# A graph-attention layer on one core: the sum of P1 and P3 taken first on VectorE in every pair of node tiles

## The chip, the core and the metric

The kernel runs on 1 core of a Trainium2 chip. The metric is the device time of one execution in microseconds (us), the median of several runs. Engines are TensorE (PE in the rows, its weight loads PEld), VectorE (DVE), ScalarE (ACT), GpSimd (POOL) and SyncE (SP), which here only issues transfers. Each engine works through its own instructions in order; between engines stand semaphores.

## What is computed

1250 nodes with 1024 features, 40,000 edges. Cut to what matters:

```python
xn = _layernorm(x)                                     # 1250 x 1024
h = xn @ L0_gnn_W                                      # 1024 x 1024: the product of this case
gnn = relu(segment_sum(h[src] * norm[:, None], dst) + b)
q, k = relu(xn @ Wq + bq), relu(xn @ Wk + bk)          # 16 heads of 64
v = xn @ Wv + bv
mix = (q @ (k.T @ v) / (1250 * 64)) @ Wo + bo          # by head; no softmax
x = x + gnn + mix
x = x + ffn(_layernorm(x))                             # quantised gate, up and down products
```

The edges are gathered and summed as a product with a matrix of edge counts. Float32 products are made of three float16 products (high x high, high x low, low x high), so each operand is split into a high half, copied by ScalarE, and a low half, the rest, taken by VectorE.

## The kernel before

The nodes are ten tiles of 128. The stages follow each other on TensorE: K and V products beside the counting of edges, Q products, then `h = xn @ gnn_W`, then Wo, then by tile the aggregation and the mix, then the feed-forward part. The change touches the third only, the stretch from 364 to 465 us.

There two tiles make a pair j (0 to 4, `PAIRS_OF_TILES`), and each pair of 2 x 2 blocks is computed with seven block products instead of eight (Winograd's form of Strassen's scheme). In TensorE's order, with the bank that each adds up in (`b0` to `b3` of `g_bank[j % 2]`, two sets of four for even and odd pairs):

| product | is | bank |
|---|---|---|
| P1 | A11 x B11 | b0, started |
| P2 | A22 x T4 | b2, started |
| P3 | S2 x T2 | b1, started |
| P4 | S1 x T1 | b3, started |
| P5 | A12 x B21 | b0, added |
| P6 | S3 x T3 | b1, added |
| P7 | S4 x B22 | b3, added |

Each is 12 matmuls of 128x512 (line 735) and raises `g_full` by one, so `g_full` reaches 7j + 3 with P3(j). As P5, P6 and P7 add onto banks whose first contents are still wanted by themselves, these are taken away before:

- `keep_p1(j)` (line 1096, ScalarE) copies b0 after P1 into `g_s1` (`p1_kept`); P5 waits for it.
- `u2(j)` (lines 1489 to 1494, VectorE) adds b1 after P3 and `g_s1` into `g_u2` (`u2`). It waits for P3(j), `p1_kept` and for `c12(j-1)`, the last reader of `g_u2`. P6 waits for it, and for the low half of S3.
- `keep_p5(j)` (line 1076, ScalarE) copies b3 after P4 into `g_s5` (`p5_kept`); it waits for P4(j) and for `c22(j-1)`. P7 waits for it.

The sums S1 to S4 of the next pair are made meanwhile. GpSimd's `s1_s3(j+1)` makes S1 and S3 (lines 519 and 522, two times three adds), VectorE's `s2` and `s4` the others (1406, 1408; 1416, 1418). ScalarE's `s_high(j,i)` (line 1060) takes the high half of Si, VectorE's `s_low(j,i)` (line 1423) the low half. After P5 to P7 the results are combined: `u3` (line 1570, needs P6), `c21` (1572), `c12` (1575, needs P7) on VectorE, `c22` (line 542) on GpSimd after `u3`; the four `h_high` (line 1069) on ScalarE and `h_low` (line 1528) on VectorE split the result. A bank of pair j is free for pair j+2 when its `h_low` or `u3` is done. GpSimd works in the order `s1_s3(j+1)`, `c22(j)`; `s1(j+1)` so comes after `c22(j-1)`.

One turn of VectorE's loop for pair j is, before the change: `s_low(j+1,1)`, `s2(j+1)`, `s_low(j+1,2)`, `s_low(j+1,3)`, `u2(j)` (for pair 0 it stands ahead of the loop), `s4(j+1)`, `s_low(j+1,4)`, `h_low` 1, `u3`, `c21`, `c12`, `h_low` 2 to 4. In the last turn, `u2(4)` is followed by the halves of Wo. One turn of ScalarE's: `keep_p1(j)`, `s_high(j+1,1)`, then for pair 0 `keep_p5(0)` and `s_high(1,2)` to `s_high(1,4)`, for the others `s_high(j+1,2)` to `s_high(j+1,4)` and then `keep_p5(j)`; then `h_high` 1 to 4. The order is written out by hand; nothing schedules it. SyncE's queue waits in this stretch for `g_full` 28 (the end of P7(3)) and then loads Wo.

Of the kernel before, what the change touches and what calls it, by code (L numbers as in the profile page):

```python
# [54 lines left out]
def gps_layer(nc, x, src, dst, gnn_W, gnn_b, Wq, bq, Wk, bk, Wv, bv, Wo, bo,  # L55
              clip_x, clip_down, w_gate, w_up, w_down, out):
    with ExitStack() as ctx:
# [208 lines left out]

        pe_slots = [(t + 1, 1) for t in range(6)] + [(6, 3), (7, 1), (8, 1), (9, 1)]
        landed = [16 * sum(1 if kind == "gu" else 2 for kind, _, _ in pieces[i % 2:i + 1:2]) for i in range(len(pieces))]
        PITCH = FB * P

# [676 lines left out]
        def _(act):  # L947
# [108 lines left out]
            def s_high(j, i):  # L1056
                act.wait_ge(SG[f"s{i}"], j + 1)
                if i == 1 and j >= 2:
                    act.wait_ge(S["g_full"], 7 * (j - 1))
                act.activation(s_half[j % 2][:, 2 * (i - 1)], s_sum[i - 1], ACT.Copy).then_inc(SG["s_hi"], 1)  # L1060
# [7 lines left out]
            def h_high(t, half, o):  # L1068
                act.activation(h16[:, half * (K // 2):(half + 1) * (K // 2), t * P:(t + 1) * P],
                               o.rearrange("p (k n) -> p k n", n=P), ACT.Copy, scale=dinv_up[:, t:t + 1]).then_inc(S["h_hi"], 1)  # L1070

            def keep_p5(j):
                act.wait_ge(S["g_full"], 7 * j + 4)
                if j > 0:
                    act.wait_ge(SG["c22"], j)
                act.activation(g_s5, g_bank[j % 2][3][:, :], ACT.Copy).then_inc(SG["p5_kept"], 1)

            def wo_high(n, c):
                act.wait_ge(SM[f"wo_in{n}_{c}"], 16)
                act.wait_ge(S["g_full"], 7 * (PAIRS_OF_TILES - 1) + (7 if n else 3))  # L1080
                act.activation(wo16[n][:, c * (K // 2):(c + 1) * (K // 2), 0, :], wo[n][c], ACT.Copy,
                               scale=W_UP).then_inc(SM["wo_hi"], 1)

            def m_high(i):
                n, p = i // PAIRS, i % PAIRS
                act.wait_ge(SM["prod_full"], i + 1)
                act.activation(m16[0][:, p, n * HALF:(n + 1) * HALF], m_bank[i % 4][:, :], ACT.Copy,
                               scale=1.0 / W_UP).then_inc(SM["m_hi"], 1)

            for j in range(PAIRS_OF_TILES):  # L1090
                last_pair = j == PAIRS_OF_TILES - 1
                b0, b1, b2, b3 = g_bank[j % 2]
                act.wait_ge(S["g_full"], 7 * j + 1)
                if j > 0:
                    act.wait_ge(SG["u3"], j)
                act.activation(g_s1, b0[:, :], ACT.Copy).then_inc(SG["p1_kept"], 1)
                if j + 1 < PAIRS_OF_TILES:
                    s_high(j + 1, 1)
                    if j == 0:
                        keep_p5(0)  # L1100
                    for i in range(2, 5):
                        s_high(j + 1, i)
                if last_pair:
                    wo_high(0, 0)
                if j > 0:
                    keep_p5(j)
                if last_pair:
                    wo_high(0, 1)
                act.wait_ge(S["g_full"], 7 * j + 5)
                act.wait_ge(SM["dinv"], 3)  # L1110
                h_high(2 * j, 0, b0[:, :])
                act.wait_ge(SG["c21"], j + 1)
                h_high(2 * j + 1, 0, b2[:, :])
                act.wait_ge(SG["c22"], j + 1)
                h_high(2 * j + 1, 1, g_c22)
                if last_pair:
                    m_high(0)
                    m_high(1)
                act.wait_ge(SG["c12"], j + 1)
                h_high(2 * j, 1, b3[:, :])  # L1120
# [77 lines left out]
        def _(dve):  # L1198
# [200 lines left out]
            def s2(j):  # L1399

                a11 = [block_at(0, 2 * j, a) for a in range(2)]
                dve.wait_ge(SG["s1"], j + 1)
                if j > 0:
                    dve.wait_ge(SG["s_lo"], 4 * j - 2)
                    dve.wait_ge(SG["s4"], j)
                dve.tensor_tensor(s_sum[1], s_sum[0], a11[0], ALU.subtract)
                dve.drain()
                dve.tensor_tensor(s_sum[1], s_sum[1], a11[1], ALU.subtract).then_inc(SG["s2"], 1)

            def s4(j):  # L1410

                a12 = [block_at(1, 2 * j, a) for a in range(2)]
                dve.wait_ge(SG["s2"], j + 1)
                if j > 0:
                    dve.wait_ge(SG["s_lo"], 4 * j)
                dve.tensor_tensor(s_sum[3], a12[0], s_sum[1], ALU.subtract)
                dve.drain()
                dve.tensor_tensor(s_sum[3], s_sum[3], a12[1], ALU.add).then_inc(SG["s4"], 1)

            def s_low(j, i):  # L1420
                dve.wait_ge(SG["s_hi"], 4 * j + i)
                high, low = [s_half[j % 2][:, 2 * (i - 1) + a] for a in range(2)]
                dve.tensor_tensor(low, s_sum[i - 1], high, ALU.subtract).then_inc(SG["s_lo"], 1)  # L1423
# [65 lines left out]
            def u2(j):  # L1489
                dve.wait_ge(S["g_full"], 7 * j + 3)  # L1490
                dve.wait_ge(SG["p1_kept"], j + 1)
                if j > 0:
                    dve.wait_ge(SG["c12"], j)
                dve.tensor_tensor(g_u2, g_bank[j % 2][1][:, :], g_s1, ALU.add).then_inc(SG["u2"], 1)  # L1494
# [26 lines left out]
            def a_tile(t, par):  # L1521
                dve.tensor_scalar(a_t[par], counts_tile(t), float(COUNT_MAX), None, ALU.min).then_inc(SB["a_ready"], 1)


            def h_low(j, i, t, half, o):
                dve.wait_ge(S["h_hi"], 4 * j + i)
                high, low = [h16[:, a * K + half * (K // 2):a * K + (half + 1) * (K // 2), t * P:(t + 1) * P] for a in range(2)]
                dve.scalar_tensor_tensor(low, o.rearrange("p (k n) -> p k n", n=P), dinv_up[:, t:t + 1], high, ALU.mult,
                                         ALU.subtract).then_inc(S["h_lo"], 1)

            def wo_low(n, c):
                dve.wait_ge(SM["wo_hi"], 2 * n + c + 1)
                high, low = [wo16[n][:, c * (K // 2):(c + 1) * (K // 2), b, :] for b in range(2)]
                dve.scalar_tensor_tensor(low, wo[n][c], W_UP, high, ALU.mult, ALU.subtract).then_inc(SM["wo_lo"], 1)
# [12 lines left out]
            for j in range(PAIRS_OF_TILES):  # L1547
                b0, b1, b2, b3 = g_bank[j % 2]
                more = j + 1 < PAIRS_OF_TILES
                if more:  # L1550
                    s_low(j + 1, 1)
                    s2(j + 1)
                    s_low(j + 1, 2)
                    s_low(j + 1, 3)
                if j > 0:
                    u2(j)
                if more:
                    s4(j + 1)
                    s_low(j + 1, 4)
                else:  # L1560
                    wo_low(0, 0)
                    wo_low(0, 1)
                    dve.wait_ge(SM["wo_lo"], 2)
                    a_tile(0, 0)
                h_low(j, 1, 2 * j, 0, b0[:, :])
                dve.wait_ge(S["g_full"], 7 * j + 6)
                if j > 0:
                    dve.wait_ge(SG["c21"], j)
                    dve.wait_ge(SG["c22"], j)
                dve.tensor_tensor(g_u3, b1[:, :], g_s1, ALU.add).then_inc(SG["u3"], 1)  # L1570
                dve.wait_ge(SG["u3"], j + 1)
                dve.tensor_tensor(b2[:, :], b2[:, :], g_u3, ALU.add).then_inc(SG["c21"], 1)
                dve.wait_ge(S["g_full"], 7 * j + 7)
                dve.wait_ge(SG["u2"], j + 1)
                dve.tensor_tensor(b3[:, :], b3[:, :], g_u2, ALU.add).then_inc(SG["c12"], 1)
                h_low(j, 2, 2 * j + 1, 0, b2[:, :])
                if not more:
                    m_low(0)
                    m_low(1)
                h_low(j, 3, 2 * j + 1, 1, g_c22)  # L1580
                h_low(j, 4, 2 * j, 1, b3[:, :])
# [216 lines left out]
```

## Time and profile before

| | us |
|---|---|
| median of 3 runs | 734.74 |
| the runs | 734.06 to 734.85 |
| the profiled execution | 733.37 |
| its span, first to last instruction | 731.3 |
| TensorE busy in it | 706.8 |
| VectorE, ScalarE, GpSimd busy | 551.0, 233.0, 347.5 |

The span is one profiled execution; 2.07 us of its time lie around the span. A difference is worked out within the profiled execution and then taken from the median. A row of a timeline names the start, the duration, the engine, the line, the operation, what is written and read, how many instructions follow each other, and in brackets the idle time before with what ended it. Rows of the timeline are merged, so that 276 matmuls can stand in one.

### The profile page before, as it was taken

The page shows a single profiled execution, that of the slowest core. Times are in us where ns is not written, and L with a number is a line of the kernel's source. Part 1 is how long each engine was busy: PE and PEld are TensorE (multiplying, and loading weights), DVE is VectorE, ACT ScalarE, POOL GpSimd, SP SyncE. Part 2 cuts the span into 40 slices and gives each one's busy share as a digit, 9 for nine tenths or more (in the row PEclk, how much of TensorE's full clock was granted, in tenths as well). Part 3 has the DMA queues.
Part 4 walks back from the last instruction along what each step waited for, and adds up shares of the span by engine and source line. Part 5 has one row for each costly group of instructions (what it writes and reads, how often), then busy time and mean ns, then how long its engine had stood idle before and what let it go on. Part 6 is the DMA issues. An engine that isn't in the chain of part 4 may idle for free.

```text
span 731.3 us, 11607 instructions
## 1 busy us (share of the span) xinstructions
PE 706.8 (97%) x3801; PEld 363.3 (50%) x3801; DVE 551.0 (75%) x1036; ACT 233.0 (32%) x382; POOL 347.5 (48%) x441
## 2 busy tenths in 40 slices
PE   4999999999999999999997999999999999999996
PEld 2455555545555554566653444444444444445753
DVE  7878887887666778875797674959977778765866
ACT  5133334553332356554323333530100000003431
POOL 4566767898666778865154440011111111113317
PEclk9999999999999999999999899999999999999999
DMA  9752412563000000000000004152322232100607
GB/s 343 220 141 63 109 37 78 158 244 119 0 0 0 1 2 1 1 0 1 1 1 0 1 0 172 59 173 66 76 88 53 55 84 66 34 12 1 116 1 280
DMA packets 52803, 52.27 MB, mean 71 GB/s; under 512 B 36514, under 2 KB 37546, under 8 KB 52752
## 3 DMA queue, kind: packets, MB, share of 16 engines
q1 hardware_dynamic: 52752, 51.61, 23.5%
q8 instruction: 30, 0.49, 0.3%
q14 instruction: 21, 0.17, 0.1%
HBM read 37.96 MB, written 5.12 MB: 59 GB/s over the span
## 4 chain that ended last, share of the span: by engine, by line
PE 75%; DVE 9%; issue 6%; ACT 2%; DMA 2%; POOL 2%; DVEq 1%; POOLq 1%; SPq 0%
PE bank L625 19%; PE bank L862 13%; PE bank L699 12%; PE bank L806 12%; PE bank L735 9%; PE bank L910 3%; PE bank L610 2%; PE bank L939 2%; PE bank L642 2%; DVE counts L1355 2%; PE bank L798 1%; DVE mem L1467 1%; ACT mem L967 1%; DMA mem<-in_L_mix_Wk 1%; POOLq L521 1%
## 5 line engine op out<-in xcount | busy, mean ns | idle before, releaser
L625 PE MATMUL bank<-mem 128*128 128x512 f16 x960 | 224.6, 383 | 2.2 <-ACT mem L967 1.7
L490 POOL TENSOR_SCALAR hot_src<-iota_p,src_col 125x128 bf16<-125x128 bf16 x252 | 186.0, 753 | 14.1 <-issue 14.1
L625 PEld LDWEIGHTS bank<-mem 128*128 128x128 f16 (+1 forms) x960 | 91.3, 98 | 99.6 <-issue 5.6
L1355 DVE TENSOR_TENSOR counts<-bank,counts 128x120 f32 x328 | 92.2, 281 | 41.8 <-PE bank L610 6.6
L862 PE MATMUL bank<-mem 128*128 128x512 f16 (+1 forms) x504 | 105.5, 369 | 0.0
L699 PE MATMUL bank<-mem 128*128 128x512 f16 (+2 forms) x576 | 105.1, 339 | 0.0
L735 PE MATMUL bank<-mem 128*128 128x512 f16 x420 | 93.8, 386 | 4.9 <-DVE mem L1494 4.9
L806 PE MATMUL bank<-mem 128*128 128x512 f16 x400 | 88.0, 379 | 0.2 <-DVE mem L1651 0.2
L862 PEld LDWEIGHTS bank<-mem 128*128 128x128 f16 x504 | 49.3, 98 | 53.7 <-issue 0.3
L699 PEld LDWEIGHTS bank<-mem 128*128 128x128 f16 (+1 forms) x576 | 55.4, 98 | 41.2
L569 POOL TENSOR_TENSOR cols<-cols 128x1 f32<-128x1 f32 x10 | 5.6, 556 | 139.1 <-DVE cols L1678 139.1
L735 PEld LDWEIGHTS bank<-mem 128*128 128x128 f16 x420 | 41.7, 100 | 56.1 <-DVE mem L1423 5.4
L1005 ACT ACTIVATE src_gap<-iota_p,loT 125x128 bf16<-125x128 bf16 x84 | 33.5, 399 | 107.8 <-PE bank L610 99.1
L806 PEld LDWEIGHTS bank<-mem 128*128 128x128 f16 x400 | 39.1, 98 | 47.4 <-issue 0.7
L487 POOL COPY src_col<-loT 125x3 f32 (+1 forms) x84 | 37.4, 445 | 47.6 <-PE bank L610 42.7
L1342 DVE TENSOR_TENSOR hot_dst<-iota_w,keyT 125x480 bf16<-125x480 bf16 x84 | 55.3, 659 | 0.0
L560 POOL TENSOR_TENSOR mem<-mem 128x1024 f32<-128x1024 f32 x10 | 23.5, 2350 | 24.7 <-DMA mem<-in_L_mix_bo 24.7
L1667 DVE SCALAR_TENSOR_TENSOR mem<-bank,mem 128x512 f32<-128x512 f32 (+1 forms) x21 | 14.0, 666 | 27.6 <-PE bank L862 26.7
L610 PEld LDWEIGHTS bank<-hot_dst,hot_src 125*128 125x128 bf16 x328 | 24.4, 97 | 20.9 <-DVE counts L1355 1.9
L1008 ACT ACTIVATE hot_src<-src_gap,cols 125x128 bf16<-125x128 bf16 x84 | 33.8, 402 | 2.7
L1281 DVE SCALAR_TENSOR_TENSOR mem<-bank,mem 128x512 f32<-128x512 f32 x40 | 27.4, 686 | 9.5 <-PE bank L625 9.5
L610 PE MATMUL bank<-hot_dst,hot_src 125*128 125x120 bf16 x328 | 30.8, 215 | 1.4 <-DVE counts L1355 0.8
(176 smaller groups left out, 829.7 us busy)
## 6 DMA issues: line engine op xcount, KB each, us to landing
mem<-in_x SPq DMA_DIRECT2D x18, 512.0 KB, 3.9
out_x<-mem SPq DMA_DIRECT2D x9, 512.0 KB
mem<-in_L_mix_Wk SPq DMA_DIRECT2D x4, 1024.0 KB, 9.6
mem<-in_L_mix_Wv SPq DMA_DIRECT2D x4, 1024.0 KB, 8.6
mem<-in_L_mix_Wq SPq DMA_DIRECT2D x4, 1024.0 KB, 5.1
mem<-in_L_gnn_W SPq DMA_DIRECT2D x4, 1024.0 KB, 7.7
mem<-in_L_mix_Wo SPq DMA_DIRECT2D x4, 1024.0 KB, 6.4
mem<-in_L_ffn_w_down SPq DMA_DIRECT2D x4, 352.0 KB, 3.1
```

What stands on the lines that cost most here:

```text
L487: pool.tensor_copy(src_col[0:EC, i, :], loT[0:EC, bass.ds(g * G, G - 1)])
L490: pool.tensor_scalar(hot_src[0:EC, i, c, :], iota_p[0:EC, :], src_col[0:EC, i, c:c + 1], None, ALU.is_equal).then_inc(S["hot_src_ready"], 1)
L610: last = pe.matmul(agg[i][:, c * WC:(c + 1) * WC], hot_src[0:EC, i, c, :], hot_dst[0:EC, i, c, :], start=(c == 0), stop=True, skip_group_c ...
L625: last = pe.matmul(o[:, :], xT[:, a * K + k, bass.ds(t * P, P)], w16[i][:, k, b, :], start=(at == 0), stop=(at == len(parts) - 1))
L699: last = pe.matmul(proj[j % 2][:, 0:w], w_q.rearrange("p a n -> p (a n)"), xT[:, a * K + k, t0 * P:t0 * P + w], start=(k == 0 and a == b), ...
L735: last = pe.matmul(o[:, :], block, g_w[right][:, k, b, :], start=(fresh and k == 0 and a == b), stop=(k == K // 2 - 1 and a == 1), skip_gr ...
L806: last = pe.matmul(agg[n][:, :], a_t[par][:, s, :], h16[:, b * K + n * (K // 2):b * K + (n + 1) * (K // 2), s * P:(s + 1) * P], start=(fre ...
L862: last = pe.matmul(o[:, 0:w], q_k, m16[b][:, k, n * HALF + c0:n * HALF + c0 + w], start=(k == 0 and a == b), stop=(k == K - 1 and a == 1))
L1005: act.activation(src_gap[0:EC, i, :], iota_p[0:EC, :], ACT.Abs, bias=loT[0:EC, bass.ds(g * G + G - 1, 1)], scale=-1.0).then_inc(S["src_gap ...
L1008: act.activation(hot_src[0:EC, i, G - 1, :], src_gap[0:EC, i, :], ACT.Relu, bias=ones[0:EC], scale=-1.0).then_inc(S["hot_src_act"], 1)
L1342: dve.tensor_tensor(hot_dst[0:EC, i], iota_w[0:EC], key, ALU.is_equal).then_inc(S["hot_dst_ready"], 1)
L1355: dve.tensor_tensor(window, agg[i][:, k * WC:(k + 1) * WC], window, ALU.add).then_inc(S["adj_added"], 1)
```

## The change

On VectorE `u2(j)` becomes the first step of the turn of pairs 1, 2 and 3 (in pair 4 it was and stays first; pair 0's stands ahead of the loop). On ScalarE `keep_p5(j)` comes directly behind `s_high(j+1,1)` for pairs 1, 2 and 3 too, as it did for pair 0; pair 4 keeps its order. No instruction is added, removed or altered, and no semaphore.

```diff
                 act.activation(g_s1, b0[:, :], ACT.Copy).then_inc(SG["p1_kept"], 1)
                 if j + 1 < PAIRS_OF_TILES:
                     s_high(j + 1, 1)
-                    if j == 0:
-                        keep_p5(0)
+                    keep_p5(j)
                     for i in range(2, 5):
                         s_high(j + 1, i)
-                if last_pair:
+                else:
                     wo_high(0, 0)
-                if j > 0:
                     keep_p5(j)
-                if last_pair:
                     wo_high(0, 1)
...
                 more = j + 1 < PAIRS_OF_TILES
+                if j > 0:
+                    u2(j)
                 if more:
                     s_low(j + 1, 1)
                     s2(j + 1)
                     s_low(j + 1, 2)
                     s_low(j + 1, 3)
-                if j > 0:
-                    u2(j)
-                if more:
                     s4(j + 1)
                     s_low(j + 1, 4)
                 else:
```

VectorE's order in turn 1, before: from the last `h_low` of pair 0 (bank1) over `s_low(2,1)`, `s2(2)` (two rows), `s_low` 2 and 3 and `u2(1)` (it reads bank6) to `s4(2)` and `s_low(2,4)`.

```order
L1528 SCALAR_TENSOR_TENSOR mem<-bank1,cols,mem 128x4x128
L1423 TENSOR_TENSOR mem<-mem 128x512
L1406 TENSOR_TENSOR mem<-mem 128x512
L1408 TENSOR_TENSOR mem<-mem 128x512
L1423 TENSOR_TENSOR mem<-mem 128x512 x2
L1494 TENSOR_TENSOR mem<-bank6,mem 128x512
L1416 TENSOR_TENSOR mem<-mem 128x512
L1418 TENSOR_TENSOR mem<-mem 128x512
L1423 TENSOR_TENSOR mem<-mem 128x512
```

The same turn after the change; line numbers are now three lower.

```order
L1525 SCALAR_TENSOR_TENSOR mem<-bank1,cols,mem 128x4x128
L1491 TENSOR_TENSOR mem<-bank6,mem 128x512
L1420 TENSOR_TENSOR mem<-mem 128x512
L1403 TENSOR_TENSOR mem<-mem 128x512
L1405 TENSOR_TENSOR mem<-mem 128x512
L1420 TENSOR_TENSOR mem<-mem 128x512 x2
L1413 TENSOR_TENSOR mem<-mem 128x512
L1415 TENSOR_TENSOR mem<-mem 128x512
L1420 TENSOR_TENSOR mem<-mem 128x512
```

`u2(1)` (line 1494, now 1491) has moved ahead of five instructions.

ScalarE's order in turn 1, before: `keep_p1(1)` (bank2), the four `s_high` in one row, `keep_p5(1)` (bank7), and the first two `h_high`.

```order
L1096 ACTIVATE mem<-bank2 128x512
L1060 ACTIVATE mem<-mem 128x512 x4
L1076 ACTIVATE mem<-bank7 128x512
L1069 ACTIVATE mem<-bank2,cols 128x4x128
L1069 ACTIVATE mem<-bank3,cols 128x4x128
```

And after, where ScalarE's line numbers are the same:

```order
L1096 ACTIVATE mem<-bank2 128x512
L1060 ACTIVATE mem<-mem 128x512
L1076 ACTIVATE mem<-bank7 128x512
L1060 ACTIVATE mem<-mem 128x512 x3
L1069 ACTIVATE mem<-bank2,cols 128x4x128
L1069 ACTIVATE mem<-bank3,cols 128x4x128
```

`keep_p5(1)` has moved ahead of three of the four `s_high`. Turns 2 and 3 differ in the same way on both engines. TensorE, GpSimd and SyncE have the same order as before.

## Rows read from the trace of the kernel before

**Rows 1.** The page, busy time of each engine (share of the span, instructions).
```profile
PE 706.8 (97%) x3801; PEld 363.3 (50%) x3801; DVE 551.0 (75%) x1036; ACT 233.0 (32%) x382; POOL 347.5 (48%) x441
```

**Rows 2.** TensorE's waits: total us, times, longest; whole span, then from 440 us.
```profile
PE bank L735 <- DVE mem L1494: 4.9, 1, 4.9
...
PE bank L892 <- DVE mem L1723: 0.6, 2, 0.4
```

**Rows 3.** Timeline of TensorE's matmuls, 355 to 480 us: start, duration, then what.
```profile
374.76 23.47 PE L735 MATMUL bank<-mem 128*128 128x512 f16 x108
403.14 62.25 PE L735 MATMUL bank<-mem 128*128 128x512 f16 x276 [4.91 <-DVE mem L1494]
```

**Rows 4.** Windows: length, busy PE, PEld, DVE, ACT, POOL, clock, DMA share, GB/s.
```profile
385.20:398.20 13.00, 13.00 (x61) 5.70 (x59) 9.66 (x14) 4.38 (x8) 7.40 (x6) 1.00 0.00 1
398.30:403.10 4.80, 0.00 (x0) 0.00 (x0) 4.03 (x6) 1.15 (x2) 1.42 (x1) 0.83 0.00 0
...
403.10:408.30 5.20, 5.16 (x13) 1.89 (x14) 2.63 (x4) 1.70 (x3) 0.00 (x0) 0.50 0.00 0
408.30:411.00 2.70, 2.70 (x14) 1.21 (x13) 1.39 (x2) 1.10 (x2) 1.79 (x2) 1.00 0.03 6
```

**Rows 5.** Timeline of VectorE, 393 to 456 us.
```profile
393.24 0.74 DVE L1528 SCALAR_TENSOR_TENSOR mem<-bank,cols,mem 128x512 f16<-128x512 f32 x1
396.32 0.96 DVE L1423 TENSOR_TENSOR mem<-mem 128x512 f16<-128x512 f32 x1 [2.34 <-ACT mem L1060]
397.20 1.64 DVE L1406 TENSOR_TENSOR mem<-mem 128x512 f32<-128x512 f32 x1
...
401.09 1.29 DVE L1423 TENSOR_TENSOR mem<-mem 128x512 f16<-128x512 f32 x2 [0.70 <-ACT mem L1060]
402.31 0.68 DVE L1494 TENSOR_TENSOR mem<-bank,mem 128x512 f32<-128x512 f32 x1
...
406.12 0.75 DVE L1528 SCALAR_TENSOR_TENSOR mem<-bank,cols,mem 128x512 f16<-128x512 f32 x1 [0.37 <-ACT mem L1069]
408.44 0.69 DVE L1570 TENSOR_TENSOR mem<-bank,mem 128x512 f32<-128x512 f32 x1 [1.57 <-PE bank L735]
...
411.03 0.70 DVE L1575 TENSOR_TENSOR bank<-bank,mem 128x512 f32<-128x512 f32 x1 [1.17 <-PE bank L735]
...
413.36 0.74 DVE L1528 SCALAR_TENSOR_TENSOR mem<-bank,cols,mem 128x512 f16<-128x512 f32 x1
...
421.15 0.68 DVE L1494 TENSOR_TENSOR mem<-bank,mem 128x512 f32<-128x512 f32 x1
...
429.16 0.70 DVE L1575 TENSOR_TENSOR bank<-bank,mem 128x512 f32<-128x512 f32 x1 [1.17 <-PE bank L735]
...
447.29 0.70 DVE L1575 TENSOR_TENSOR bank<-bank,mem 128x512 f32<-128x512 f32 x1 [1.17 <-PE bank L735]
...
455.06 0.69 DVE L1494 TENSOR_TENSOR mem<-bank,mem 128x512 f32<-128x512 f32 x1 [5.10 <-PE bank L735]
```

**Rows 6.** Timeline of ScalarE, 392 to 456 us.
```profile
392.88 0.58 ACT L1096 ACTIVATE mem<-bank 128x512 f32<-128x512 f32 x1
395.65 0.63 ACT L1060 ACTIVATE mem<-mem 128x512 f16<-128x512 f32 x1 [2.19 <-POOL mem L522]
400.43 1.15 ACT L1060 ACTIVATE mem<-mem 128x512 f16<-128x512 f32 x2 [4.15 <-DVE mem L1408]
...
404.93 0.58 ACT L1076 ACTIVATE mem<-bank 128x512 f32<-128x512 f32 x1
...
455.12 1.91 ACT L1081 ACTIVATE mem<-mem 128x2048 f16<-128x2048 f32 x1 [4.64 <-PE bank L735]
```

**Rows 7.** Timeline of GpSimd, 392 to 415 us.
```profile
392.90 2.72 POOL L522 TENSOR_TENSOR mem<-mem 128x512 f32<-128x512 f32 x2
...
409.21 1.27 POOL L542 TENSOR_TENSOR mem<-mem 128x512 f32<-128x512 f32 x1 [9.36 <-DVE mem L1570]
...
411.74 2.72 POOL L522 TENSOR_TENSOR mem<-mem 128x512 f32<-128x512 f32 x2
```

## The prediction

> **What bounds the kernel now.** I read the page first, then TensorE's waits, then the time around the one long wait, engine by engine. The page says that TensorE is busy for 706.8 of 731.3 us [rows 1], so a change elsewhere can only bring what TensorE stands still or runs slowly. The view of its waits has one long entry after the start-up: 4.9 us, once, before line 735, released by VectorE's line 1494, which is `u2` [rows 2]. Line 735 is all seven products of all five pairs, 12 matmuls each. I write P6(1) for the sixth product of pair 1, and count as the code does (pairs 0 to 4). The timeline shows where the wait lies [rows 3]: 108 matmuls, which are P4(0) to P5(1), run from 374.76 to 398.23; then nothing until 403.14; then 276 matmuls, P6(1) to P7(4), with no gap. So the wait is at P6(1), the first product that needs `u2(1)`, and the other `u2`s were in time. The windows show a second loss [rows 4]: the granted clock is 1.00 before the pause (2.4 GHz), falls while TensorE stands still, is 0.50 (1.2 GHz) from 403.1 to 408.3 after it, and then 1.00 again.
>
> Why is `u2(1)` late? VectorE ran it at 402.31, behind `s_low(2,1)` (396.32), `s2(2)` (two adds from 397.20 on) and `s_low(2,2)`, `s_low(2,3)` (401.09, two instructions) [rows 5]. What it needs was there long before: P3(1) ended two products of 2.61 us (23.47 / 9 [rows 3]) before P5(1) did, at 398.23 - 5.22 = 393.0; `keep_p1(1)` ran from 392.88 to 393.46 on ScalarE [rows 6]. VectorE ended pair 0 with the `h_low` at 393.24, at 393.98, and then sat idle for 2.34 us until ScalarE's first copy, which itself waited for GpSimd's `s1(2)` [rows 5 to 7].
>
> **The change, part by part.** No instruction is added or removed and SP's and GpSimd's queues are untouched; two are moved, and only for pairs 1, 2 and 3.
>
> 1. `u2(1)` on VectorE, one add of 0.68 us [rows 5]. It now stands ahead of `s_low(2,1)` and can start at 394.0 and end at 394.7. That is inside the idle 2.34 us, so `s_low(2,1)` still starts at 396.32: cost nothing. If that cover were gone it would cost 0.7 us on VectorE, and P6(1) would still be served. P6(1) can start when P5(1) ends, at 398.23, with 3.5 us to spare. Gain on TensorE: 4.91 us.
>
> 2. The clock after the pause. P6(1) ran from 403.14 until VectorE's line 1570, released by it, at 408.44 [rows 3, 5]: 5.3 us. A product at full clock takes 2.59 us: line 1575, which waits for P7 of each pair, is released at 411.03, 429.16 and 447.29, 18.13 us apart for seven products [rows 5]. The difference is 2.7 us; the window of 5.2 us at 0.50 gives 2.6 [rows 4]. Without the pause I expect the clock to stay up, as it does in the 13 us before it [rows 4]. The bounds are 0 (the clock falls for another reason) and 2.7; I take 2.7, since the fall lies within the pause in the trace and nowhere else near. The Trainium skill, "TensorE: Matmul & The Clock Gate", section "What's actually happening", says that the throttled clock is the default and that activity releases it, which gives the sum with the clock term; a clock that had nothing to do with activity would give the sum without it. It also says that the moment of release differs from run to run, so that this term could differ between executions.
>
> 3. `keep_p5(1)` on ScalarE, one copy of 0.58 us [rows 6]. It must move too: before, it ran at 404.93, behind `s_high(2,2)` to `s_high(2,4)`, and P7(1) waits for it. P7(1) is now due at 398.23 + 2.59 = 400.8; with `u2` alone moved, P7(1) would wait until about 405.5 and nearly the whole gain would be gone. In its new place behind `s_high(2,1)` (395.65 to 396.28) it ends at 396.9 (P4(1) had ended at 395.6), 3.9 us early. What stands behind it on ScalarE, `s_high(2,2)`, came at 400.43 because of VectorE [rows 6]; the 4.15 us of idle time before it hide the copy.
>
> 4. Added waits. `u2(j)` at the head of VectorE's turn now makes everything behind it wait for P3(j): `s_low(j+1,1)`, `s2`, `s4`, and then this pair's `h_low`, `u3`, `c21`, `c12`. I follow pair 2. VectorE's turn 1 ran from 396.32 to 414.10 (the `h_low` at 413.36 and its 0.74). Out of it fall the waits for TensorE (1.57 us before line 1570, 1.17 before line 1575), `u2` itself (0.60 until the next start) and 0.37 for ScalarE behind its late copy: 3.7 us, so that it ends at 410.4 and is 14.1 us long [rows 5]. P3(2) ends at 398.23 + 5 x 2.59 = 411.2. So VectorE waits 0.8 us and `u2(2)` ends at 411.9; P6(2) is due at 416.4, 4.5 us later. Meanwhile `s_low(3,1)` cannot start before GpSimd's `s1(3)`: its `c22(1)` started at 409.21 behind `u3(1)` and will start about 2.6 us sooner (`u3(1)` follows the `h_low` of 406.12 to 406.87, which itself moves up by 0.60 + 0.37: 405.9 instead of 408.44), so `s1(3)` ends near 411.9 instead of 414.46 [rows 7] and `s_low(3,1)` is possible from 412.6. The wait at `u2(2)` thus ends ahead of it and costs nothing. In pair 3 P3(3) ends 18.13 us after P3(2), at 429.3. VectorE has ended its turn at 412.6 + 14.1 = 426.7 and waits 2.6 us; `s_low(4,1)`, one lap of 16.3 us after 412.6 if nothing else held it, was possible at 428.9 and starts at 430.0, so the chain loses 1.1 us. Nobody is waiting for it: the first product that needs it is P3(4), which starts at 444.9, and `s_low(4,2)` is done 5.4 us after `s_low(4,1)` starts (396.32 to 401.7 in pair 2), at about 435.4. The cover of `u2(j)` itself is always P4(j) and P5(j), 5.2 us, against 0.7.
>
> `keep_p5(2)` waits for P4(2), 413.8, while `s_high(3,2)` comes 4.1 us after `s_low(3,1)` (396.32 to 400.43 in pair 2), at 416.7, so it hides too; for pair 3 the two are 431.9 and 434.1. The nearest other term is `keep_p1(2)` for P5(2): done at about 410, due at 413.8.
>
> 5. Pair 4 is not changed. VectorE waited 5.10 us for P3(4) before `u2(4)` and ScalarE 4.64 us for it before its copy of Wo [rows 5, 6]; both keep counting from P3(4), and the Wo loads are issued at the end of P7(3), so all of this moves up with TensorE. From 440 us on TensorE's own waits are 2.4 us in all, the largest entry 0.6 us (six entries) [rows 2]: there is no bound in the rest that could swallow the gain.
>
> Sum, on the profiled execution: 733.37 - 4.91 - 2.70 = 725.8 us (span 731.3 - 7.6 = 723.7, and 2.1 around it). That execution is 1.4 us below the median of the runs, 734.74; taken from the median the same 7.6 us give **727.1 us**, 1.0% less.
>
> **The rivals.**
> (a) Only the idle time goes and the clock still falls for about as long. For it: no other row near shows what the clock does in a pause this long. Against it: 1.00 in the densely used 13 us before. Time: 734.74 - 4.9 = 729.8 us.
> (b) A new, shorter wait at a later product, because TensorE now arrives 7.6 us sooner and VectorE, ScalarE and GpSimd only some 3 to 4 us sooner. The pairs in question are 2 and 3. For it: with pair 2 in the old order `u2(2)`, which ended at 421.83 [rows 5], could come only some 3 us sooner, near 419, against 416.4, so it is the order in pair 2 that decides. Against it: the margins of 3.5 to 5 us worked out above. A wait of 1 to 4 us, with no or part of the clock loss, gives 728 to 733; I take 730.5.
> (c) The change doesn't do what it says: the pause goes from P6(1) to P7(1), if `keep_p5(1)` is still late because `s_high(2,1)` ahead of it waits for GpSimd. It decides when `s1(2)` comes more than 3.9 us later than now. Then about 734 us again.
> (d) Slower: VectorE's wait for P3(j) at the head of its turn throws the chain of the next pair behind TensorE. Place: `s_low(j+1,2)` for P3(j+1). It decides when VectorE's turn from `u2(j)` to there, 6 us by my count, takes more than the 15.5 us that TensorE needs for six products; or when the whole turn, 14.8 us with `u2` at its head, outgrows 18.13 us by the 5.2 us of cover. Price: a stop like the present one (4.9 + 2.7 us) in pairs 2 and 3 each, less the one removed: 734.74 + 7.6 = 742.3 us.
>
> **How the numbers follow.** The forecast 0.83, (a) 0.04, (b) 0.05, (c) 0.04, (d) 0.04. The time is the forecast's, 727.1. For the range: 0.8 us either way for the spread of the runs shown (734.06 to 734.85), 0.7 more below for small waits on VectorE that may go as well, and above it reaches over (a) and to the middle of (b): 725.4 to 730.5. 0.2% of this kernel is 1.5 us, about what a measurement can tell from no change: faster than that are the forecast, (a) and (b), 0.92; within it is (c), 0.04; slower is (d), 0.04.
>
> **What would show it.** In the changed kernel's profile TensorE's waits should have no entry between line 735 and `u2` above 0.3 us; the product rows should be one run of matmuls from `max_T`'s transpose to P7(4), ending near 457.8 instead of 465.4; the granted clock should be 1.00 in every window from 364 to 490; `u2(1)` should start near 394.0 without a wait, `u2(2)` and `u2(3)` should wait for TensorE by 0.8 and 2.6 us; `keep_p5(1)` should run near 396.3. The forecast is wrong if TensorE still stops at P6 or P7 of any pair, if the clock dips without a stop, or if a wait of some us appears after 458 us that is not there now.

## The result, and the profile after

| | before | after |
|---|---|---|
| median, us | 734.4 | 727.29 |
| lowest to highest | 734.06 to 734.85 (4 runs) | 725.91 to 729.05 (4 runs) |
| profiled execution | 733.37 | 727.32 |
| its span | 731.3 | 725.2 |
| TensorE busy in it | 706.8 | 704.7 |

The ratio is 0.9909, 95% interval 0.9895 to 0.9923: 6.7 us less (5.6 to 7.7). The forecast was 727.1 us and 7.6 us less.

TensorE's timeline from 364 us on, of the kernel after, beside [rows 3]:

```profile
364.26 5.34 PE L735 MATMUL bank<-mem 128*128 128x512 f16 x24
369.83 2.39 PE L757 MATMUL bank<-cols,mem 128*128 128x1 f32 x20 [0.22 <-DVEq L1473]
372.08 4.13 PE L735 MATMUL bank<-mem 128*128 128x512 f16 x12
376.01 0.42 PE L773 MATMUL bank<-ident,cols 128*1 128x128 f32 x1
376.22 83.29 PE L735 MATMUL bank<-mem 128*128 128x512 f16 x384
459.34 2.90 PE L798 MATMUL bank<-mem 128*128 128x512 f16 x12
```

P4(0) to P7(4) are now one run of 384 matmuls (108 + 276 before). The view of TensorE's waits no longer has an entry for line 735 at all. The windows around the old pause, beside [rows 4], have the full clock:

```profile
385.20:398.20 13.00, 13.00 (x62) 5.88 (x60) 9.56 (x15) 5.87 (x10) 6.10 (x6) 1.00 0.00 1
398.20:403.40 5.20, 5.20 (x26) 2.35 (x24) 4.43 (x5) 1.15 (x2) 2.80 (x2) 1.00 0.00 0
403.40:411.00 7.60, 7.60 (x37) 3.43 (x36) 6.64 (x11) 3.61 (x6) 3.08 (x3) 1.00 0.01 2
```

VectorE in turns 1 to 4, beside [rows 5] (`u2` is line 1491 now, `s_low` 1420):

```profile
395.19 0.67 DVE L1491 TENSOR_TENSOR mem<-bank,mem 128x512 f32<-128x512 f32 x1
397.61 0.96 DVE L1420 TENSOR_TENSOR mem<-mem 128x512 f16<-128x512 f32 x1 [1.75 <-ACT mem L1060]
...
412.93 0.69 DVE L1491 TENSOR_TENSOR mem<-bank,mem 128x512 f32<-128x512 f32 x1 [1.55 <-PE bank L735]
413.71 0.97 DVE L1420 TENSOR_TENSOR mem<-mem 128x512 f16<-128x512 f32 x1
...
431.05 0.69 DVE L1491 TENSOR_TENSOR mem<-bank,mem 128x512 f32<-128x512 f32 x1 [3.58 <-PE bank L735]
...
449.18 0.69 DVE L1491 TENSOR_TENSOR mem<-bank,mem 128x512 f32<-128x512 f32 x1 [4.91 <-PE bank L735]
```

`u2(1)` lies in the old idle time, `u2(2)` and `u2(3)` wait for TensorE, and TensorE for neither.

**Where the profiled execution lost 1.5 us again.** P3(0), the 12 matmuls at 372.08, took 4.13 us; before, the row read `372.06 2.75`. The next run starts at 376.22 instead of 374.76. It is the clock, in a place that the change doesn't touch. First the kernel after, then the kernel before, same window:

```profile
374.00:375.00 1.00, 1.00 (x4) 0.32 (x3) 1.00 (x2) 0.00 (x0) 0.94 (x1) 0.50 0.00 0
```
```profile
374.00:375.00 1.00, 1.00 (x7) 0.50 (x6) 1.00 (x2) 0.00 (x0) 0.96 (x1) 1.00 0.00 0
```

Before it TensorE had done nothing but the ten pairs of one-column matmuls of the node degrees (2.39 us, line 757). The books of the stretch: 384 matmuls from 376.22 to 459.34 are 83.1 us against 90.5 us before (374.76 to 465.22, pause included), 7.3 us less; 1.5 us lost at P3(0); together 5.9 of the 6.1 us by which the span is shorter. Of the changed kernel two profiles were taken (the second in the experiments), and both show this fall (4.13 and 4.16 us); the one profile of the kernel before does not. How often it comes in the other executions of either kernel no run shows.

### The profile page after: what moved, and what is told of

It reads as the page before. It is cut to its first block, busy times and chain, and to the rows that moved or that the text cites. A ratio compares the mean times of both kernels' runs of the same rounds, so it can differ in the third digit from the quotient of the medians.

```text
span 725.2 us, 11607 instructions
## 1 busy us (share of the span) xinstructions
PE 704.7 (97%) x3801; PEld 362.7 (50%) x3801; DVE 550.3 (76%) x1036; ACT 232.5 (32%) x382; POOL 348.0 (48%) x441
## 4 chain that ended last, share of the span: by engine, by line
PE 80%; DVE 10%; issue 4%; ACT 2%; DVEq 1%; POOL 1%; DMA 1%; POOLq 0%; SPq 0%
PE bank L625 18%; PE bank L862 14%; PE bank L699 12%; PE bank L735 12%; PE bank L806 12%; PE bank L910 3%; PE bank L610 2%; DVE mem L1464 2%; DVE mem L1238 2%; PE bank L939 2%; PE bank L642 2%; DVE counts L1352 2%; PE bank L798 1%; ACT mem L967 1%; DMA mem<-in_x 1%
## 5 line engine op out<-in xcount | busy, mean ns | idle before, releaser
L490 POOL TENSOR_SCALAR hot_src<-iota_p,src_col 125x128 bf16<-125x128 bf16 x252 | 186.0, 754 | 14.1 <-issue 14.1
```

Of the source, the lines that this page charges most:

```text
L490: pool.tensor_scalar(hot_src[0:EC, i, c, :], iota_p[0:EC, :], src_col[0:EC, i, c:c + 1], None, ALU.is_equal).then_inc(S["hot_src_ready"], 1)
```

## The experiments

All times are medians of several executions; each group ran on one chip with the kernel before beside it (734.4, 734.0 and 734.7 us, 7 to 18 executions). The first question was whether each of the two moves was needed, and for which pairs.

**VectorE's half alone.**

```diff
+                if j > 0:
+                    u2(j)
                 if more:
                     s_low(j + 1, 1)
...
-                if j > 0:
-                    u2(j)
-                if more:
                     s4(j + 1)
```

> VectorE's half of the change alone: u2(j) first, ScalarE's keep_p5(j) still behind the four s_high. My theory (P6 waits for u2, P7 for keep_p5, both had to move): the stop goes from P6(1) to P7(1). P7(1) is due at 400.8 us and keep_p5(1) ends near 404.9, so about 4.1 us of pause and up to 2.6 us of half clock; and as u2(2) and u2(3) now tie VectorE's chain to P3(j), keep_p5(2) and keep_p5(3) come late too, 1 to 2 us each. Total 734 to 738 us, so no gain or a loss. Rival (VectorE's order is what matters, ScalarE's copy had slack): 727 to 728 us, like the full change.

Measured: 732.49 us (731.7 to 734.05), ratio 0.9973 (0.9962 to 0.9984). The stop is at P7(1) now, as its releaser shows, ScalarE's line 1076, `keep_p5`; rows of TensorE, ScalarE and VectorE:

```profile
376.13 26.06 PE L735 MATMUL bank<-mem 128*128 128x512 f16 x120
405.94 58.84 PE L735 MATMUL bank<-mem 128*128 128x512 f16 x264 [3.75 <-ACT mem L1076]
```
```profile
405.30 0.58 ACT L1076 ACTIVATE mem<-bank 128x512 f32<-128x512 f32 x1
...
424.78 0.58 ACT L1076 ACTIVATE mem<-bank 128x512 f32<-128x512 f32 x1
```
```profile
398.17 1.64 DVE L1406 TENSOR_TENSOR mem<-mem 128x512 f32<-128x512 f32 x1
...
418.20 0.69 DVE L1494 TENSOR_TENSOR mem<-bank,mem 128x512 f32<-128x512 f32 x1 [5.10 <-PE bank L735]
418.80 0.68 DVE L1423 TENSOR_TENSOR mem<-mem 128x512 f16<-128x512 f32 x1
419.40 0.68 DVE L1406 TENSOR_TENSOR mem<-mem 128x512 f32<-128x512 f32 x1
```

120 matmuls instead of 108 stand before the stop. It costs 3.75 us. At the full clock a row of n matmuls here takes n x 0.2158 + 0.16 us (108 in 23.47, 120 in 26.06, 276 in 59.73 in the run with the filled pause below), so the 264 behind the stop would need 57.1 us and took 58.84: 1.7 us of clock. With 3.75 that is 5.5 of the 7.4 us that the rows give for the old stop (4.91 and 2.5, as shown below); 2.0 are left, and 734.4 - 2.0 = 732.4. The place of the stop was right, and the rival is out. My 734 to 738 us were too pessimistic: I had `keep_p5(2)` late too. It was in time by 0.6 us (it ended at 425.36; P7(2) was due three products, P4 to P6, after P3(2)'s end at 418.2, at 426.0). I had taken `s2(3)` at its duration beside GpSimd's adds (1.64 us for its first add [rows 5], and again at 398.17 here); this time it ran when GpSimd had been done for 2 us, in 0.68 us. From its start to its second add's end `s2` took 3.20 us in pair 1 and 1.45 us in pair 2; with the longer time the copy would have ended 1.75 us later, 1.1 us too late.

**ScalarE's half alone**, shown against the kernel before.

```diff
                     s_high(j + 1, 1)
-                    if j == 0:
-                        keep_p5(0)
+                    keep_p5(j)
                     for i in range(2, 5):
...
```

> ScalarE's half alone: keep_p5(j) early, u2(j) at its old place behind s_low(j+1,3). My theory: P6(1) still waits for u2(1) at 402.3 us, the pause of 4.9 us and the half clock after it stay, 733.5 to 735 us, no change. Rival (ScalarE's late copy held VectorE's chain and so u2): the pause shrinks by more than 1 us and the time falls below 733.

Measured: 735.65 us (734.57 to 737.0), ratio 1.0017 (1.0006 to 1.0028): a little slower than before, and above my 733.5 to 735. The pause did not shrink by more than 1 us (4.50 us, 4.91 before), so the rival is out. Three stops stand where one did:

```profile
376.78 23.47 PE L735 MATMUL bank<-mem 128*128 128x512 f16 x108
404.76 21.21 PE L735 MATMUL bank<-mem 128*128 128x512 f16 x84 [4.50 <-DVE mem L1491]
426.61 18.29 PE L735 MATMUL bank<-mem 128*128 128x512 f16 x84 [0.64 <-DVE mem L1491]
445.53 23.47 PE L735 MATMUL bank<-mem 128*128 128x512 f16 x108 [0.64 <-DVE mem L1491]
```

The first is the old one at P6(1). The two of 0.64 us, at P6(2) and P6(3), I had not foreseen. Rows of ScalarE, then of VectorE, tell how they come about:

```profile
423.42 0.60 ACT L1076 ACTIVATE mem<-bank 128x512 f32<-128x512 f32 x1 [6.66 <-PE bank L735]
423.91 1.14 ACT L1060 ACTIVATE mem<-mem 128x512 f16<-128x512 f32 x2
```
```profile
424.56 1.29 DVE L1420 TENSOR_TENSOR mem<-mem 128x512 f16<-128x512 f32 x2 [3.69 <-ACT mem L1060]
425.77 0.69 DVE L1491 TENSOR_TENSOR mem<-bank,mem 128x512 f32<-128x512 f32 x1
```

`keep_p5(2)` waits for P4(2), and `s_high(3,2)`, `s_low(3,2)`, `s_low(3,3)` and `u2(2)` queue up behind it: 3.1 us from the end of P4 (423.4) to that of `u2` (426.5), while only P5, 2.6 us, lies between P4 and P6. With `u2` at its late place the early `keep_p5` puts `u2` behind P4. So the halves depend on each other both ways.

**Both moves, pair 1 alone.**

```diff
-                    if j == 0:
-                        keep_p5(0)
+                    if j <= 1:
+                        keep_p5(j)
...
+                if j == 1:
+                    u2(j)
...
-                if j > 0:
+                if j > 1:
                     u2(j)
```

> Both moves for pair 1 alone; pairs 2 and 3 in the old order. My theory: the pause at P6(1) goes, TensorE then arrives at P6(2) at about 416.4 us while u2(2) comes at about 418.4 to 419.1, so a new stop of 2.7 us there, none in pair 3: 2.7 us above the full change if the clock holds, 5.3 if it falls, 729.9 to 732.6 us. Rival (only pair 1 ever stopped, so only pair 1 had to move): 727 to 728 us.

Measured: 731.87 us (730.13 to 732.46), ratio 0.995 (0.9934 to 0.9966).

```profile
376.93 41.60 PE L735 MATMUL bank<-mem 128*128 128x512 f16 x192
421.03 43.09 PE L735 MATMUL bank<-mem 128*128 128x512 f16 x192 [2.50 <-DVE mem L1494]
```

192 matmuls are 16 products, P4(0) to P5(2): the stop is at P6(2), 2.50 us (expected 2.7), and none follows in pair 3. The 192 behind it take 43.09 us against 41.60 of the row before it, 1.5 us more. 2.5 + 1.5 above 727.3 is 731.3. Pair 2 never stopped before, but only since TensorE arrived there late.

**`u2` early everywhere, `keep_p5` early for pairs 0 and 1 alone.**

```diff
-                    keep_p5(j)
+                    if j <= 1:
+                        keep_p5(j)
                     for i in range(2, 5):
                         s_high(j + 1, i)
+                    if j > 1:
+                        keep_p5(j)
```

> u2(j) first in all pairs as in the change, keep_p5(j) early for pairs 0 and 1 only, late for 2 and 3. My theory: P7(2) is due at 419 to 420.3 us, keep_p5(2) behind s_high(3,4) ends about 2.0 us later, so one stop of 2 us there with 1.5 to 2 us of half clock, none in pair 3: 3 to 4 us above the changed kernel, 730 to 731.5 us. Rival (once the first stop is gone ScalarE's copy has slack, as it had in pairs 2 and 3 of the run with VectorE's half alone): 727 to 728 us.

Measured: 729.54 us (728.28 to 730.31), ratio 0.9935 (0.9918 to 0.9951).

```profile
374.73 44.19 PE L735 MATMUL bank<-mem 128*128 128x512 f16 x204
421.03 39.02 PE L735 MATMUL bank<-mem 128*128 128x512 f16 x180 [2.11 <-ACT mem L1076]
```

One stop of 2.11 us at P7(2), as expected (2.0). The median is below my 730 to 731.5. In the profiled execution the clock fell neither behind the stop (the 180 matmuls took 39.02 us, 39.0 being the full clock) nor at P3(0) (2.75 us). But of the four executions that one was the fastest, 728.28 us at a mean clock of 0.998; the others took 729.39 to 730.31 us at 0.993 to 0.997, and where the clock fell in them isn't shown.

**A middle place for `u2`**, the changed kernel otherwise.

```diff
-                if j > 0:
+                if j > 0 and not more:
                     u2(j)
                 if more:
                     s_low(j + 1, 1)
                     s2(j + 1)
+                    if j > 0:
+                        u2(j)
                     s_low(j + 1, 2)
...
```

> A middle place: u2(j) of pairs 1 to 3 behind s2(j+1), ahead of s_low(j+1,2); keep_p5 early. u2(1) then runs at about 400.4 to 401.1 us against 398.2 at which P6(1) is due: my theory gives one pause of 2.9 us there and none in pairs 2 and 3. 2.9 us above the changed kernel if the clock holds in so short a pause, 730.0; up to 5.5 above if it falls, 732.6. Rival (any place ahead of s4 is good enough): 727 to 728 us.

Measured: 731.72 us (730.57 to 732.06), ratio 0.996 (0.9947 to 0.9973).

```profile
376.83 23.47 PE L735 MATMUL bank<-mem 128*128 128x512 f16 x108
402.84 61.42 PE L735 MATMUL bank<-mem 128*128 128x512 f16 x276 [2.54 <-DVE mem L1491]
```

One stop of 2.54 us at P6(1) (expected 2.9), and 276 matmuls in 61.42 us, 1.7 us over 59.73. Three places of `u2`, all with `keep_p5` early, thus give three stops of P6(1): 4.50 us (old place), 2.54, none.

**The clock's share by itself.** The kernel before with 20 more matmuls in the pause:

```diff
                 product(j, (0, 1), "B21", b0, False)
+                if j == 1:
+                    pe.wait_ge(S["h_lo"], 4)
+                    pe.wait_ge(SG["s_lo"], 8)
+                    for _ in range(20):
+                        pe.matmul(g_bank[0][2][:, :], s_half[1][:, 4, 0, :], g_w["B11"][:, 0, 0, :],
+                                  start=True, stop=True, skip_group_check=True)
```

> The kernel before with 20 extra matmuls of 128x512 put on TensorE directly ahead of P6(1), into a bank that P2(2) starts anew, so that TensorE works (4.3 us at full clock) while it would wait for u2(1). Nothing is left out. My theory (the pause itself lets the clock fall): the clock stays at 1.00, P6(1) starts as late as before but runs at 2.59 instead of 5.3 us: 2.6 to 2.7 us faster than before, 731.6 to 732.2 us. Rival (the clock falls for another reason at that point): 734 to 735 us with 0.50 in the windows after 403 us.

Measured: 731.31 us (731.03 to 732.54), ratio 0.9956 (0.9939 to 0.9974), 3.2 us less (1.9 to 4.5) for 20 matmuls more.

```profile
374.76 23.47 PE L735 MATMUL bank<-mem 128*128 128x512 f16 x108
398.07 4.48 PE L785 MATMUL bank<-mem 128*128 128x512 f16 x20
403.14 59.73 PE L735 MATMUL bank<-mem 128*128 128x512 f16 x276 [0.59 <-DVE mem L1500]
```

P6(1) starts at 403.14, exactly as before, and the same 276 matmuls take 59.73 instead of 62.25 us [rows 3]. The clock is 1.00 from 403 to 408 us. That is the clock's term of the sum, 2.5 us by the rows (2.7 predicted), and it hangs on what TensorE did in the pause: rival (a) of the prediction is out.

**The changed kernel again.**

> The changed kernel itself once more, beside the next two on the same chip, to see how its executions spread (725.9 to 729.1 us so far, with mean clocks of 0.999 to 0.994). My theory: the spread is the clock, which falls in some executions around the ten pairs of 128x1 matmuls at 370 us or in the start-up; time and mean clock of the executions lie on one line, about 3.6 us for 0.005. Median 726 to 728 us. Rival: the spread has nothing to do with the clock.

Measured: 727.32 us (725.83 to 727.73), ratio 0.99 (0.9885 to 0.9914). The two series of the change, eight executions, with the mean granted clock of each:

```
us      725.83 725.91 727.26 727.27 727.32 727.38 727.73 729.05
clock    0.999  0.999  0.997  0.997  0.995  0.995  0.997  0.994
```

The fastest have the highest clock and the slowest the lowest; between them the order is loose (727.73 at 0.997). That fits the clock as the cause of most of the spread; only two of the eight have a profile, and the one line of time against clock that I had expected is not there.

**The degree products, singly between matmuls of P3(0).**

```diff
                 if j == 0:
                     pe.wait_ge(SM["sources"], 1)
-                    for n in range(T):
-                        last = pe.matmul(agg[0][:, n:n + 1], sources[:, n * P:(n + 1) * P], ones, start=True, stop=True,
-                                         skip_group_check=True)
-                    last.then_inc(SM["deg_full"], 1)
...
+                        if (j, left) == (0, 2) and n < T:
+                            degree(n)
+                            n += 1
```

> The changed kernel, with the ten 128x1 products of the node degrees (2.4 us in one piece between P2(0) and P3(0)) put singly behind the first ten matmuls of P3(0). My theory (the stretch of nothing but one-column matmuls can let the clock fall for some 3 us, as in the profile of the change, 1.4 us lost): the fall there disappears, the mean time is 0 to 1.5 us below the changed kernel and no window from 370 to 380 us is below 1.00. Rival (that fall is not due to these matmuls): same times, the fall is seen there as often.

Measured: 730.55 us (726.96 to 732.46), 3.2 us above the change run beside it. A failure, with a plain cause:

```profile
364.26 5.34 PE L742 MATMUL bank<-mem 128*128 128x512 f16 x24
371.76 0.38 PE L742 MATMUL bank<-mem 128*128 128x512 f16 x1 [2.15 <-DVE mem L1426]
```
```profile
371.70:379.00 7.30, 7.24 (x33) 5.86 (x34) 4.34 (x4) 0.63 (x1) 6.73 (x6) 0.53 0.00 0
379.00:381.00 2.00, 2.00 (x7) 0.83 (x6) 1.26 (x5) 0.00 (x0) 2.00 (x2) 0.50 0.00 0
```

The degree products had covered a wait of P3(0) for `s_low(0,2)`. Behind the bare stop nearly all of P3(0) and the degree products ran at 1.2 GHz (0.53 on average), and so did the next 3 us of full products: the window from 381 to 382 us still has 0.50. The stop itself (2.15 us) is no longer than the one piece of degree products that stood there (2.39 us), so most of the loss is the clock's; the one of the six executions with a mean clock of 0.998 took 726.96 us. The run can't answer its question, whether the clock stays up when one-column matmuls are placed singly, since here it had a stop ahead of them. So P5(0), which needs neither sum, was put in as new cover, with `keep_p1(0)` ahead of `s_high(0,4)` and two counts of `g_full` adapted:

```diff
+                if j == 0:
+                    pe.wait_ge(SG["p1_kept"], 1)
+                    product(0, (0, 1), "B21", b0, False)
+                    pe.wait_ge(SM["sources"], 1)
...
-                act.wait_ge(S["g_full"], 7 * j + 4)
+                act.wait_ge(S["g_full"], 7 * j + (4 if j else 5))
...
-                dve.wait_ge(S["g_full"], 7 * j + 3)
+                dve.wait_ge(S["g_full"], 7 * j + (3 if j else 4))
```

**P5(0) early, degree products singly in P3(0).**

> The changed kernel with pair 0 in another order: P1(0), P2(0), P5(0), then P3(0) with the ten one-column degree products put singly between its matmuls, then P4, P6, P7; keep_p1(0) goes ahead of s_high(0,4). P5(0) now covers the wait for s_low(0,2) that the degree products covered in the changed kernel (the run with interleaving alone stopped there for 2.15 us). Nothing is left out. My theory (what lets the clock fall near 370 us is a stretch in which TensorE stands or runs one-column matmuls only): no stop and no window from 364 to 384 us below 1.00, about 726 us in nearly every execution, 0 to 1.5 us below the changed kernel's median of 727.3. Rival (one-column matmuls let the clock fall however they are mixed): the fall is still there, and lasts longer, 727.5 to 729.5 us.

Measured: 724.9 us (724.66 to 725.26, 4 executions), ratio 0.9869 (0.9853 to 0.9886). Its window, and its longest run of matmuls:

```profile
364.00:380.00 16.00, 16.00 (x92) 9.09 (x90) 15.10 (x21) 5.10 (x10) 7.98 (x7) 1.00 0.01 1
```
```profile
376.46 80.45 PE L742 MATMUL bank<-mem 128*128 128x512 f16 x372
```

**P5(0) early, degree products in one piece**, the control:

> As the other one with P5(0) early, but the ten degree products in one piece of 2.4 us between P5(0) and P3(0). Control for it: by my theory the fall of the clock shows in as many executions as in the changed kernel, 726 to 727.5 us by execution; the other order of the products alone brings nothing. Rival (the order of pair 0 matters by itself): a median more than 1 us off the changed kernel's 727.3.

Measured: 725.91 us (725.06 to 726.68, 4 executions), ratio 0.9878 (0.9861 to 0.9895).

```profile
371.87 2.29 PE L730 MATMUL bank<-cols,mem 128*128 128x1 f32 x20
374.02 4.44 PE L742 MATMUL bank<-mem 128*128 128x512 f16 x12
```
```profile
364.00:380.00 16.00, 16.00 (x79) 8.25 (x78) 12.76 (x16) 4.51 (x9) 8.51 (x7) 0.89 0.00 0
```

Behind the piece of one-column matmuls P3(0) took 4.44 us, as in the changed kernel; with them spread out the clock stayed up in the profiled execution, and all four executions lie within 0.6 us. The singly placed version is 9.6 us below before by its ratio, and 0.3 to 0.4% below the change by theirs. It is also 1.1 us below the 726 that I had expected, and the control's median lies 1.4 us below the change's, where I had named more than 1 us as the sign of my rival, that the order of pair 0 matters by itself. The change run ran on another chip, but the rows show a part of it:

```profile
364.10 7.93 PE L742 MATMUL bank<-mem 128*128 128x512 f16 x36
```

From the end of this row of the control, 372.03, to P3(0) pass 1.99 us; in the changed kernel, from 369.60 to 372.08, 2.48 us. The degree products now follow without the 0.22 us of idle time and take 2.29 us instead of 2.39. So the other order brings 0.5 us by itself in these profiles, and the rest of the 1.4 us isn't explained. Nor is all of the step from the control to the singly placed version the clock: in the two profiles 2.5 us lie between them from the first product to Wo's (92.1 and 94.6 us), of which P3(0) at the lower clock is 1.7 (4.44 against 2.75); by the medians the step is 1.0 us, with intervals of the ratios that overlap.

## Why the prediction was right

- **Step 1, `u2(1)` in VectorE's idle time: right.** It started at 395.19 (394.0 predicted; everything was 1.2 to 1.5 us late behind P3(0)), cost nothing, and P6(1) no longer stops. The run with VectorE's old order (ScalarE's half alone) keeps a stop of 4.50 us.
- **Step 2, the clock: right in kind, 2.5 us instead of 2.7** by the run with the filled pause. With 4.91 that makes 7.4 us; the two long runs of matmuls say 7.3. The 0.2 us too much come from the sum's 5.3 us for P6(1), which ran to the release of line 1570 and so holds the 0.16 us that every row has behind its last matmul, while the 2.59 us taken off it does not; a single product at the full clock is a row of 2.75 us. That the size may differ from execution to execution is not tested for this stop, of which there is one profile; other stops in other runs differ, with 1.7 and 1.5 us of clock behind 2.54 and 2.50 us, and none behind 2.11 us.
- **Step 3, `keep_p5(1)` must move too: right.** Without it the stop went to P7(1). "Nearly the whole gain would be gone" was too strong; 2.0 of 7.4 us stayed, as that stop is 3.75 us long with 1.7 us of clock lost behind it. In the changed kernel the copy ran at 397.48 (396.3 predicted), in time.
- **Step 4, the added waits cost nothing: right, though the waits were longer than worked out.** `u2(2)` and `u2(3)` waited 1.55 and 3.58 us (0.8 and 2.6 predicted). `u2(2)` was released at 412.93, 1.7 us after the 411.2 of the sum, most of it the fall at P3(0), while VectorE was ready at 411.37, only 1.0 us after its 410.4: its turn began 1.3 us late but took 13.8 us (397.61 to 411.37), not 14.1. Even 5.10 us of such waiting, in the run with VectorE's half alone, held up TensorE nowhere, which leaves rival (d) no ground here.
- **Pair 2 needs the moves, though it did not stop before: right.** Left in the old order it stops for 2.50 us at P6(2), or with `keep_p5` alone left late for 2.11 us at P7(2). That is what rival (b) would have looked like. For pair 3 it is not shown: it did not stop in either run, but the stop in pair 2 had made TensorE late for it, and no run leaves pair 3 alone in the old order.
- **Step 5, nothing in the rest swallows the gain: right.** From the start of Wo's products (465.22 before, 459.34 after) the rest of the span differs by 0.2 us.
- **What the sum lacked** is a term in a place that the change leaves alone: the fall of the clock behind the one-column matmuls, 1.5 us in the profile of the change and not in that of before. The prediction had named 1.00 in every window from 364 to 490 us as a sign that it holds, and a dip of the clock without a stop as one that it is wrong; this dip came, without a stop, and for the same reason the products ended at 459.5 instead of 457.8. The waits, the order and the clock behind the old stop came out as forecast all the same; the sign was drawn too wide, since the change does not touch that place. The range's 0.8 us for the spread was meant for such things; 729.05 us, the slowest execution, shows that for single executions it was narrow. The lower bound was also added up wrongly: 727.1 - 0.8 - 0.7 is 725.6, not 725.4.
- **That the time came within 0.2 us is in part luck.** The sum took 7.6 us off 734.74, the median of three runs; with the fourth the median is 734.4. The ratio says 6.7 us less, so 0.9 us too much was taken off a base that was 0.3 us too high, and the median of the four runs of the change lies 0.4 us below what the ratio gives.

## What to carry to other kernels

Ask of every long wait on the bounding engine what stands ahead of the late instruction on its engine, and whether that needed to be ahead; then follow the same chain for the next product, and for the next iterations as they arrive earlier. Two moves that are each worth little or less than nothing can be worth all of it together: test a pair of moves in halves before dropping either. Before spreading out or moving small work on the bounding engine, look for the wait that it covers.

## What the runs showed of the hardware that I had not expected

- Stops of TensorE of 2.50 and 2.54 us, and one of 2.15 us, were already followed by matmuls at half the clock, while one of 2.11 us was not. The half clock also followed, in most profiles, on 2.3 to 2.4 us of 128x1 matmuls during which TensorE counts as busy: P3(0) behind them took 4.13 to 4.44 us instead of 2.75 in seven of the profiles, and 2.75 us in those of before, of the filled pause and of the run with `keep_p5` early for pair 1 alone.
- Twenty additional 128x512 matmuls in a pause made the kernel 3.2 us faster (1.9 to 4.5; 2.5 by the rows), without anything else being moved.
- The same add on VectorE, two float32 operands in SBUF, 128x512, took 1.64 us beside GpSimd's adds [rows 5] (`396.88 2.98 POOL L522`, two adds) and 0.68 us when GpSimd was idle. The Trainium skill, "SBUF — State Buffer", section "SBUF: two separate sides", has the two engines share one pair of ports that a VectorE instruction with two SBUF inputs and a GpSimd one hold in turn; these rows agree, and my estimate for VectorE's half alone went wrong for that reason.
